# Nested branches, and both parts of a front piece at one place of a head, in an attention kernel

## The reference

```python
q = x * rotation_params[None, :, None, :]
k = x * entangle_params[None, :, None, :]
attn_scores = jnp.einsum('bhid,bhjd->bhij', q, k) * scale
attn_weights = jax.nn.softmax(attn_scores, axis=-1)
out = jnp.einsum('bhij,bhjd->bhid', attn_weights, x)
...
x = x + _layernorm(_L0_attn_ref(_layernorm(x), ...))
x = x + _layernorm(_L0_ffn_ref(_layernorm(x), ...))   # r, k, v products, a token shift, relu squared
x = x + _layernorm(_L1_attn_ref(_layernorm(x), ...))  # linear attention and an MLP with gelu
x = x + _layernorm(_L1_ffn_ref(_layernorm(x), ...))   # silu(gate) * up, down
```

## Time and profile before

| | us |
|---|---|
| median of 3 runs | 3142.48 |
| lowest, highest | 3142.14, 3146.02 |
| the profiled execution, own time | 3144.77 |
| its span, first to last instruction | 3142.9 |
| TensorE busy (products) | 2878.9 |
| ScalarE busy | 2400.7 |
| VectorE busy | 1400.3 |
| GpSimd busy | 226.3 |

### The profile page before, as it was taken

The page is one execution under the profiler, slowest core; times in us unless marked ns, Lnnn a source line. Parts: engine busy times, 40 slices in busy tenths (PEclk is TensorE's granted clock), DMA queues, the critical chain, the costliest instruction groups (busy, mean ns, idle before and its releaser), DMA issues. The chain is left out here.

```text
span 3142.9 us, 48524 instructions
## 1 busy us (share of the span) xinstructions
PE 2878.9 (92%) x18320; PEld 1156.1 (37%) x18320; DVE 1400.3 (45%) x3422; ACT 2400.7 (76%) x2672; POOL 226.3 (7%) x194
## 2 busy tenths in 40 slices
PE   1998998999999999999999999669999999999996
PEld 0221221222222222222222222146666666666664
DVE  6231230322432233223330132276778888865675
ACT  2999999999999999999999999734444444543432
POOL 0000000000000000000000000011211111210110
PEclk9999999999999999999999999879999999999998
DMA  3411110310210211111120111121122211211110
GB/s 118 141 44 33 55 49 29 92 56 26 82 56 26 78 63 56 50 50 41 57 72 25 36 39 42 51 74 54 54 68 86 61 60 60 73 48 49 38 47 21
DMA packets 125602, 177.71 MB, mean 57 GB/s; under 512 B 42248, under 2 KB 100616, under 8 KB 125128
## 3 DMA queue, kind: packets, MB, share of 16 engines
q1 hardware_dynamic: 122392, 172.53, 17.0%
q10 hardware_dynamic: 2992, 2.23, 0.2%
HBM read 107.62 MB, written 67.11 MB: 56 GB/s over the span
## 5 line engine op out<-in xcount | busy, mean ns | idle before, releaser
L718 ACT ACTIVATE probs<-ps 128x1024 f32<-128x1024 f32 x2048 | 1894.3, 1168 | 86.9 <-PE ps L457 83.3
L586 PE MATMUL ps<-probs,vals 128*32 128x512 f32 x8192 | 1094.4, 607 | 0.0
L457 PE MATMUL ps<-qT,kT 64*128 64x512 f16 x4096 | 730.5, 387 | 109.3 <-DMA kT<-split_dram 27.0
L457 PEld LDWEIGHTS ps<-qT,kT 64*128 64x128 f16 x4096 | 173.6, 93 | 1151.2 <-ACT probs L718 1024.9
L586 PEld LDWEIGHTS ps<-probs,vals 128*32 128x32 f32 x8192 | 162.0, 108 | 294.8 <-issue 233.2
L873 DVE COPY sums<-ps 128x512 f32<-128x512 f32 x64 | 44.3, 692 | 503.2 <-PE ps L586 503.2
L1642 ACT ACTIVATE gate<-layers_ps 128x512 f32<-128x512 f32 x96 | 57.2, 596 | 252.1 <-DVE gated L1864 149.3
L1352 PE MATMUL layers_ps<-weight_mem,hT 128*128 128x256 f32 x1024 | 230.8, 380 | 0.0
L1352 PEld LDWEIGHTS layers_ps<-weight_mem,hT 128*128 128x128 f32 x1024 | 193.0, 190 | 29.9 <-ACT hT L1615 1.2
L1479 PE MATMUL layers_ps<-yT,weight_mem 128*128 128x512 f16 x768 | 173.3, 380 | 13.6 <-ACT hT L1615 13.6
L1505 PE MATMUL layers_ps<-n4T,weight_mem 128*128 128x512 f16 x768 | 177.0, 386 | 6.6 <-DVE y_out L1705 4.3
(11 more groups left out here) (237 smaller groups left out, 2602.7 us busy)
## 6 DMA issues: line engine op xcount, KB each, us to landing
split_dram<-parts SPq DMA_DIRECT2D x28, 768.0 KB, 3.7
qT<-split_dram SPq DMA_DIRECT2D x126, 128.0 KB
kT<-split_dram SPq DMA_DIRECT2D x126, 128.0 KB
heads_dram<-result SPq DMA_DIRECT2D x64, 128.0 KB, 7.4
q_in<-q_dram SPq DMA_DIRECT2D x16, 512.0 KB, 3.3
n_in<-n_dram SPq DMA_DIRECT2D x16, 512.0 KB, 3.6
x_in<-x_dram SPq DMA_DIRECT2D x16, 512.0 KB, 5.2
out_dram<-y_out SPq DMA_DIRECT2D x16, 512.0 KB, 4.2
```

The lines of the kernel that those rows point to most:

```text
L457: last = nc.tensor.matmul(SCORES[slot][:, n * BANK:(n + 1) * BANK], kT[buf][rows, j * P:(j + 1) * P], qT[buf][rows, q0:q0 + BANK], start=T ...
L586: mm = nc.tensor.matmul(ACC[32 * c:32 * c + 32, :], vals[buf][:, j, :], probs[:, j % PROBS, c * BANK:(c + 1) * BANK], start=(j == 0), stop ...
L718: nc.scalar.activation(probs[:, j % PROBS, half * T // 2:(half + 1) * T // 2], SCORES[slot_of(at)], ACT.Exp, scale=OPERAND_SCALE ** -2).th ...
```

## The change

`PART_GAP` goes from 3 to 0, so that `next_scores` runs part 0 and part 1 of a piece directly behind each other, both behind the first score half of the place's key block.

The five branches, which followed each other, are nested. The flag now says that the unit is safe (`is_le` in place of `is_gt`). The `If` arm holds the fast code of unit i, then the load of the next flag and the next branch, and in the innermost one the second half of the last head. The `Else` arm holds the general code of all units from i on. So the program contains the general code of 64, 56, 48, 32 and 16 heads in five copies, where before it had it once.

```diff
-PART_GAP = 3
+PART_GAP = 0
...
-            for i, unit in enumerate(UNITS):
+            def units_from(i):
+
                 pe.wait_ge(flags_ready, i + 1)
                 pe.sem_inc(waited, 1)
-                is_general = pe.value_load(flags[0:1, i:i + 1], min_val=0, max_val=1)
-                with pe.If(is_general > 0):
-                    unit_of_heads(unit, True)
+                is_safe = pe.value_load(flags[0:1, i:i + 1], min_val=0, max_val=1)
+                with pe.If(is_safe > 0):
+                    unit_of_heads(UNITS[i], False)
+                    if i + 1 < len(UNITS):
+                        units_from(i + 1)
+                    else:
+                        second_half(NHD - 1, False)
                 with pe.Else():
-                    unit_of_heads(unit, False)
-            second_half(NHD - 1, False)
+                    for unit in UNITS[i:]:
+                        unit_of_heads(unit, True)
+                    second_half(NHD - 1, False)
+
+            units_from(0)
...
-                    ch.link(V.tensor_scalar(flags[:, unit:unit + 1], widest[:, 1, :], SAFE, None, ALU.is_gt))
+                    ch.link(V.tensor_scalar(flags[:, unit:unit + 1], widest[:, 1, :], SAFE, None, ALU.is_le))
...
-            for i, unit in enumerate(UNITS):
-                is_general = dve.value_load(flags[0:1, i:i + 1], min_val=0, max_val=1)
+            def units_from(i):
+
+                is_safe = dve.value_load(flags[0:1, i:i + 1], min_val=0, max_val=1)
                 steps_done = fch.n
-                with dve.If(is_general > 0):
-                    unit_of_heads(unit, True)
+                with dve.If(is_safe > 0):
+                    unit_of_heads(UNITS[i], False)
+                    if i + 1 < len(UNITS):
+                        units_from(i + 1)
+                    else:
+                        second_half(NHD - 1, False)
                 fch.n = steps_done
                 with dve.Else():
-                    unit_of_heads(unit, False)
-            second_half(NHD - 1, False)
+                    for unit in UNITS[i:]:
+                        unit_of_heads(unit, True)
+                    second_half(NHD - 1, False)
+
+            units_from(0)
             dve.wait_ge(weights_ready, 3)
```

## The result

| | before | after |
|---|---|---|
| median, us | 3142.72 | 3149.01 |
| lowest, highest | 3139.22, 3147.34 | 3146.07, 3151.63 |
| runs | 20 | 20 |
| span of the profiled execution | 3142.9 | 3146.2 |

The changed kernel takes 1.0019 times the time of the one before, with a 95% interval of 1.0012 to 1.0026: 6.3 us more, where I had forecast 23.6. All times of one comparison come from the same chip. 3149 is the number of rival (a), in which the five exits cost what one costs; it gave 3151.

The account below looks back on a forecast made before the run. ScalarE's exponentials plus its stalls were taken to bound the attention stage. Terms -15.7 (branches), +15.3 (way out) and +24 (pairs) sum to +23.6 us, giving a median of 3166 us, range 3149 to 3178.

Parts of the forecast that it names:

- rival (a): Way out of the nested branches: exits folded into one, or cheap, adding 0 in place of +15.3; 3151 us, chance 0.12.
- What bounds the kernel: Attention stage: lasts as long as ScalarE's exponentials plus its stalls, mostly waits for TensorE's score product; the barrier moves the end.
- Step 1: Branches at heads 7, 15, 31, 47: fast arm in place saves 19.2 us of stalls, 3.5 left for the rest; -15.7 us.
- Step 2: End of the attention stage: TensorE makes five far jumps in a row, 3.67 us each, moving the barrier; +15.3 us.
- Step 3: Both parts at one key block: 52 pairs at about 0.95 us cost 52, late parts worth 28 go; net +24 us.
- Rival (b): Pairs of parts: the three score buffers absorb them, so step 3 adds 0; 3142 us, chance 0.06.

Follow-up runs that it names:

- nest_only: The changed kernel with PART_GAP back at 3, so only the branches are nested; 3126.42 us, ratio 0.9948 to the kernel before.
- nest_five_exits: `nest_only` with one semaphore increment behind each of the five nested If/Else on TensorE and VectorE; 3144.91 us, ratio 1.0007 to the kernel before.
- gap0_only: The kernel before with PART_GAP 0 alone, its branches not nested; 3164.26 us, ratio 1.0069 to the kernel before.
- flat_fast_first: The kernel before with the arms exchanged, fast code in the If arm, branches still one after the other; 3147.72 us, ratio 1.0011.

## Why the prediction was wrong, point by point

| step of the prediction | forecast | measured |
|---|---|---|
| 1, the branches in the middle | -15.7 | -15.9 (stage, `nest_only`) |
| 2, the way out | +15.3 | +0.9 (last exponential to barrier) |
| 3, both parts at one place | +24 | +23.2 (stage, after against `nest_only`) |
| start of the stage, not in the forecast | 0 | -2.0 |
| sum | +23.6 | +6.2 (barrier); the medians differ by +6.3 |

The table adds up to the barrier of two profiled executions. The medians hold as well what lies behind the barrier (2.9 us less in these two, of it 1.7 by the clock at one place), and the start, which follows no edit. That both sums come to about 6 is in part luck.

**What bounds the kernel: right.** Every move of the stage's end was ScalarE's time plus ScalarE's stalls. The price of a stall was wrong: I took a shown stall of x as x + 0.10 and the distance of exponentials as 0.92 us. The 0.92 holds for the first one behind a stall; the others follow at 0.904, and what a stall costs beyond the shown x depends on how long the row in front of it is (0.30 us at the first stall of the pair in head 20).

**Step 1: right**, in mechanism and size. The branches go on in place in 65 ns, the clock no longer falls, and the order at key blocks 8 and 9 leaves its stalls. I had left 3.5 us for them; taking that order away gave 2.7. The 4.8 us a head is right (head 7 took 34.17 us, a plain head 29.33), though the 26.7 us for 29 exponentials should have been 26.2.

**Step 2, "The way out": this is the step that failed.** I wrote: "From the innermost body the fast path makes five jumps in a row, each over thousands of TensorE instructions." It makes one. The price was not the mistake: one exit is 3630 ns, inside my 3.5 to 3.85, and `nest_five_exits` shows five of them on the path when they exist. The count was. I counted source blocks, while the sequencer runs what the compiler leaves. Behind the innermost arm's end there is no instruction but the next arm's jump, four times over, and the trace has one row for all of them. That the compiler joins jumps which lead to jumps is inferred from this and from the five rows of `nest_five_exits`; the compiled program itself was not read. (My upper bound for this step is a slip too: five at 3.85 give +16.1, not 16.5.) I had this as rival (a), with its price, and gave it 0.12, since "against it, 3740 ns on the one exit over a body". That row was no evidence against it: it tells what an exit costs and nothing of how many are left. The evidence on the count was in my own front text, that the arm's jump is left out where its target is the next instruction: a compiler that does this looks at where jumps lead. On that I should have put (a) near even.
The one exit is hidden for the most part, as the forecast had it for (a). VectorE arrives last, at 2019.4; it leaves its own arm at 2016.4 and stands 3 us. Its row shows 51 ns and the time is in the gap behind it, while TensorE's row holds the time itself. Not all of the 0.9 us is the exit's: SyncE is done 7.1 us behind the last exponential's start, where it was 6.6, and why is open.

The profile shows the price of a far target as a row of 3.3 to 4.9 us, against 65 to 89 ns in place. The Trainium skill ("Runtime: NRT & Kernel Launch", "Instruction fetch mechanics") says that a taken branch out of the fetched pages must first bring its target in; the trace agrees, and the rule applies to a jump that is executed. The Trainium skill ("Advanced Engine Details and Errata", "Control Flow Timing") has about 51 ns for a branch-always; no far jump here is near it, so by that page the right total would have come for a wrong reason.

**Step 3: right in mechanism and in the net**, 23.2 (24), with the distance of the halves at 2.25 (2.24) and the two stalls shown as 0.41 and 0.35. **The two terms of the net were both too small.** From start to start a pair costs 1.18 us and not 0.95, and the two late parts that go cost 0.34 each, 0.68 a piece, where my 28 us are 0.54. Both errors come from the same overlap, and in the difference they nearly cancel (0.50 us a piece against my 0.41). That much was luck. The 0.15 us for the semaphore in that sum was an estimate without a row; single rows of the trace put 0.18 to 0.23 between the start of an exponential and the score half that its predecessor releases (1173.10 and 1173.31, for one). Rival (b), that the score buffers absorb the pair, fell with `gap0_only`.

**The start.** In the profiled executions the first exponential starts between 63.9 and 67.8 us, behind the DMA of kT. `gap0_only` and the kernel before jump at 56.6 and 56.4 alike and start at 65.5 and 67.7; `flat_fast_first` doesn't jump there and starts at 63.9, `nest_only` doesn't either and starts at 67.7. It isn't the first branch; what it is stays open.

**The range.** 3149 to 3178 ended where the result is. It reached over (a) with hardly anything to spare, for an alternative that differed from the forecast by 15 us and that no row spoke against.

## What to carry to other kernels

Nest run-time branches with the usual case in the arm that follows in place, and keep nothing between the ends of the nested blocks: each of the branches then costs a fall-through, and the end costs one far jump; one instruction behind each of the five brought all five jumps back. Before pricing a control-flow change, count the jumps that will be executed, not the blocks in the source. Work slipped into an engine that is ahead by 0.3 us a block costs more in one lump (1.18 us a piece here) than in two parts three blocks apart (0.68); and the lead is no account to save in, since the buffers between the engines bound it: here even a lone part cost 0.34 us. To price such stalls, count from start to start and not the idle time that is shown.

## What the runs showed of the hardware that I had not expected

Far jumps of TensorE directly behind each other are dearer than single ones: 3315 ns for the first of the five, 4549, 4671, 4892 and 4556 for the next, where all single ones in these runs took 3.3 to 4.3 us. VectorE's five start at 1994.8, 1997.7, 2001.2, 2004.9 and 2008.6, and its block ends at 2012.1: 2.9, 3.4, 3.8, 3.6 and 3.5 us, so there too the first is the cheapest. I had priced five at the same 3.67. Whether the target's distance or the short way since the last jump makes it was not tried.

TensorE's clock in the same 25 us (columns as in the earlier trace rows) is near its lower level while the sequencer stands in jumps, and at it in the first products of the later layers:

```profile
1993.00:2018.00 25.00, 0.66 (x4) 0.42 (x4) 1.93 (x4) 0.00 (x0) 0.10 (x1) 0.55 0.07 15
2018.00:2022.00 4.00, 1.27 (x6) 1.30 (x7) 1.66 (x10) 0.00 (x0) 0.00 (x0) 0.50 0.38 86
```

The second row is not the doing of the five jumps: the changed kernel, with one exit, has a clock of 0.55 behind its barrier too (2019 to 2023).

In the middle of the stage a jump can cost more than its standstill. At head 7 of the kernel before, 4.8 us were lost in all, and 1.1 after nesting (30.4 us from the head's first exponential to the next head's, where an undisturbed head takes 29.3). Of the 3.7 that went, 2.0 is the first stall (2.34 to 0.37), and 1.8 are the two behind it, which stood in the stretch at a clock of 0.62. In the middle of the stage the low clock came with each such standstill and with nothing else, in every kernel here, so how much of the 1.8 is the clock's was not separated.
